# Attention loop of a decoder layer: how the moments, roots and shifts of its two normalisations are formed

## The chip, the cores and the metric

The kernel runs on one core of a Trainium2 chip. The metric is the time of one execution on the device, in microseconds.

## The reference, cut to what matters

The input x is 128 sequences of 64 rows with 128 features, fp32. A layer of three parts is computed on it, each with a layer normalisation in front:

```python
x = x + attn(_layernorm(x), wq, bq, ..., wo, bo)          # linear attention, 16 heads of 8
x = x + xattn(_layernorm(x), ctx_1024, ...)               # autocorrelation attention, 5 lags
x = x + ffn(_layernorm(x), norm_scale, w_router, ...)     # 2 of 8 experts

def _layernorm(x, axis=-1, eps=1e-05):
    m = jnp.mean(x, axis=axis, keepdims=True)
    v = jnp.var(x, axis=axis, keepdims=True)
    return (x - m) / jnp.sqrt(v + eps)
```

The first attention passes q and k through `x + 1` where x is positive and `exp(x)` elsewhere, sums the outer products of keys and values along the sequence, and divides `q * S` by `q * z`. The change concerns the first normalisation and the second.

## The kernel before, in words

The 8192 rows are 64 tiles of 128 rows (a tile is two sequences), and 4 tiles make a group, so there are 16 groups. X stays on the chip. Each engine has a program of its own, written by hand, and waits on semaphores; no planner orders the work. The attention loop goes by slots, n from -3 to 17: slots -3 to 3 and 12 to 17 are written out, slots 4 to 11 run under a loop counter, two to a turn. In a slot several groups are worked on, each at another stage (`stage(n, i, shift)` gives the group n + shift, or nothing):

- shift 3 (`z`): VectorE takes the statistics of X for the first normalisation, `bn_stats` over each of four tiles (`st_a`, line 883) and `bn_aggr` (`mv_a`, line 891), which gives mean and variance; GpSimd makes variance + eps (`ve`), its power -0.5 (`rs`, line 529), mean times root (`mr`) and 1 - that (`nb`, line 542).
- shift 2: ScalarE forms `xh = rs * x + nb` (line 688). That 1 is taken out again by the weights.
- shift 1: TensorE transposes `xh` (line 1353), ScalarE copies it (`xT`), TensorE projects tile by tile, ScalarE takes each projection out (`ex`, `rl`, `v`, lines 674 to 679), GpSimd adds `ex` and `rl` (`qk`, line 551) and forms the outer products (line 560).
- shift 0: TensorE makes the running sums (`run`), VectorE multiplies them by q (`R`, line 906) and sums them (`num`, line 916). The sums of tile 0 are made at the end of the slot before.
- shift -1 (`c`): VectorE divides (`on`, line 961), TensorE transposes `on` and projects it, VectorE adds it to X (line 969) and takes the statistics of the second normalisation (`st_c`, `mv_c`). GpSimd makes `ve_c` and `rs_c` in this slot.
- shift -2: GpSimd makes `mr_c` and `nb_c`, ScalarE forms `xh2` (line 688), TensorE transposes it and multiplies it with the projected context; ScalarE stores the result as `gd` (line 733).

The orders of VectorE and TensorE in a slot matter here. VectorE: R0, num0, reciprocal, R1, `on`, `st_a`, key products, `mv_a`, num1, sums, R2, num2, add to X, R3, `st_c`, num3, `mv_c`. TensorE: transposes of `xh`, sums 1, projection 0, key sums, projection 1, transposes of `on`, sums 2, context keys, output projection, projection 2, transposes of `xh2`, sums 3, projection 3, sums 0 of the next group, gram. In slot -3 VectorE goes on, behind the statistics of group 0, to the folding of the weights and the splitting of the biases, and only then to group 1. ScalarE in a slot: copy `xT`, projection 0, `oT`, projection 1, `xh2`, `k2T` and `x2T`, projection 2, denominators, `xh`, projection 3, `gd`. After slot 17 VectorE makes half of the last `xh2` itself (line 1041) and reduces the diagonals (line 1057).

Of the kernel before, what the change touches and what calls it, by code (L numbers as in the profile page):

```python
# [9 lines left out]
ALU = mybir.AluOpType  # L10
# [3 lines left out]
P = 128  # L14
# [52 lines left out]
def build(nc, x, ctx_t, ctx_r, wqkv_p, b_all, wo, wq2, wk2, wv2t, wo2, bq2, bk2, bv2, scale, w_router, w_experts,  # L67
          tri, stri, ident, iota, dest, walk, place, late_in, out):
    with ExitStack() as ctx:
# [48 lines left out]
        power = sb("power", [P, GT])  # L118
# [5 lines left out]
        st_a, mv_a = sb("st_a", [P, GT, 6]), [sb(f"mv_a{i}", [P, GT, 2]) for i in range(2)]  # L124
        ve_a, rs_a = sb("ve_a", [P, GT]), [sb(f"rs_a{i}", [P, GT]) for i in range(2)]
        mr_a, nb_a = sb("mr_a", [P, GT]), [sb(f"nb_a{i}", [P, GT]) for i in range(2)]
# [16 lines left out]
        st_c, mv_c = sb("st_c", [P, GT, 6]), [sb(f"mv_c{i}", [P, GT, 2]) for i in range(2)]  # L143
        ve_c, rs_c = sb("ve_c", [P, GT]), [sb(f"rs_c{i}", [P, GT]) for i in range(2)]
        mr_c, nb_c = sb("mr_c", [P, GT]), [sb(f"nb_c{i}", [P, GT]) for i in range(2)]
# [91 lines left out]
        def psum(name, banks=1):  # L237
# [18 lines left out]
        a_st, a_mv, a_ve, a_rs, a_xh = sem("a_st"), sem("a_mv"), sem("a_ve"), sem("a_rs"), sem("a_xh")  # L256
        a_ex = sem("a_ex")
        a_mr, a_nb, c_mr, c_nb = sem("a_mr"), sem("a_nb"), sem("c_mr"), sem("c_nb")
# [5 lines left out]
        c_den, c_rden, c_on, c_tr, c_oT, c_y, c_x1, c_st, c_mv, c_ve, c_rs = (  # L264
            sem(n) for n in ("c_den", "c_rden", "c_on", "c_tr", "c_oT", "c_y", "c_x1", "c_st", "c_mv", "c_ve", "c_rs"))
# [58 lines left out]
        def stage(n, i, shift):  # L324

            if i is None and not 0 <= n + shift < NG:
                return None
            return grp(n + shift, i)

# [175 lines left out]
        def _(pool):  # L505
# [12 lines left out]
            def variance(g, p, stats, seen, ve, ve_sem, rs, rs_sem, normed):  # L518

                need(pool, rs_sem, g)  # L520
                pool.wait_ge(seen, GT * g + GT)
                settle(pool)
                nc.gpsimd.tensor_scalar(ve[:], stats[p][:, :, 1], 1.0, LN_EPS, ALU.mult, ALU.add).then_inc(ve_sem, 1)

            def root(g, p, stats, seen, ve, ve_sem, rs, rs_sem, normed):

                pool.wait_ge(ve_sem, g + 1)
                need(pool, normed, GT * (g - 1))
                nc.gpsimd.tensor_tensor(rs[p][:], ve[:], power[:], ALU.pow).then_inc(rs_sem, 1)

            def mean_times_root(g, p, mv, rs, rs_sem, mr, mr_sem, nb_sem):

                pool.wait_ge(rs_sem, g + 1)
                need(pool, nb_sem, g)
                nc.gpsimd.tensor_tensor(mr[:], mv[p][:, :, 0], rs[p][:], ALU.mult).then_inc(mr_sem, 1)

            def shift(g, p, mr, mr_sem, nb, nb_sem, normed):

                pool.wait_ge(mr_sem, g + 1)
                need(pool, normed, GT * (g - 1))  # L540
                settle(pool)
                nc.gpsimd.tensor_scalar(nb[p][:], mr[:], -1.0, 1.0, ALU.mult, ALU.add).then_inc(nb_sem, 1)
# [20 lines left out]

            def slot(n, i):
                z, a1, c, d = (stage(n, i, k) for k in (3, 1, -1, -2))
                of_z = z and (z[0], z[1], mv_a, a_mv, ve_a, a_ve, rs_a, a_rs, a_xh)
                of_c = c and (c[0], c[1], mv_c, c_mv, ve_c, c_ve, rs_c, c_rs, d_xh)
# [4 lines left out]
                if d:  # L572
                    mean_times_root(d[0], d[1], mv_c, rs_c, c_rs, mr_c, c_mr, c_nb)
                    shift(d[0], d[1], mr_c, c_mr, nb_c, c_nb, d_xh)
                if a1:
                    outer_product(*a1, 0)
                    features(*a1, 1)
                    outer_product(*a1, 1)
                    features(*a1, 2)
                if z:  # L580
                    variance(*of_z)
                if a1:
                    outer_product(*a1, 2)
                if z:
                    root(*of_z)
                if a1:
                    features(*a1, 3)
                if z:
                    mean_times_root(z[0], z[1], mv_a, rs_a, a_rs, mr_a, a_mr, a_nb)
                if c:  # L590
                    variance(*of_c)
                if z:
                    shift(z[0], z[1], mr_a, a_mr, nb_a, a_nb, a_xh)
                if a1:
                    outer_product(*a1, 3)
                if c:
                    root(*of_c)
# [63 lines left out]
        def _(act):  # L661
# [23 lines left out]
            def norm(g, p, rs, nb, nb_sem, dst, dst_sem, own=GT):  # L685
                act.wait_ge(nb_sem, g + 1)
                for k in range(own):
                    nc.scalar.activation(dst[:, k, :], X[:, bass.ds(GT * g + k, 1), :].rearrange("p a b -> p (a b)"),
                                         ACT.Identity, bias=nb[p][:, k:k + 1], scale=rs[p][:, k:k + 1]).then_inc(dst_sem, 1)

            def slot(n, i):
# [1070 lines left out]
```

## Time and profile before

| | us |
|---|---|
| median of 3 runs (lowest, highest) | 621.97 (621.57, 622.45) |
| the profiled execution | 619.28 |
| its span, first to last instruction | 617.4 |
| busy: TensorE, VectorE, GpSimd, ScalarE | 553.1, 504.5, 419.3, 391.7 |

PE is TensorE's matmul, PEld its weight load, DVE VectorE, ACT ScalarE, POOL GpSimd. The span covers the profiled execution from its first instruction to its last; the execution's own time is 1.9 us longer. In a timeline row the first number is the start, the second the duration, both in us; a bracket gives the idle time of the engine just before and what ended it. Durations of neighbours on one engine overlap a little, so what an instruction costs its engine is read from its start to the next one's start. Busy shares are averages over stages that are bound by different things.

### The profile page before, as it was taken

How to read it: one execution, taken by the hardware profiler on the slowest of the kernel's cores; microseconds unless marked ns; L12 is line 12 of the kernel's file. 1: busy time of each engine (PE TensorE's matmuls, PEld its weight loads, DVE VectorE, ACT ScalarE, POOL GpSimd, SP SyncE). 2: the span in 40 equal slices, each digit the busy share in tenths (PEclk: the TensorE clock that was granted, in tenths of full speed). 3: DMA queues.
4: the chain of work that ended last, by engine and by line, in shares of the span. 5: the costliest groups of instructions: out<-in, count | busy, mean ns of one | idle time of the engine just before them, and what ended most of it. 6: DMA issues, size and time to landing. Idle time of an engine off the chain costs nothing.

```text
span 617.4 us, 16339 instructions
## 1 busy us (share of the span) xinstructions
PE 553.1 (90%) x4286; PEld 407.0 (66%) x4287; DVE 504.5 (82%) x1504; ACT 391.7 (63%) x1030; POOL 419.3 (68%) x523
## 2 busy tenths in 40 slices
PE   4888999999999997778999788999999999999993
PEld 1333444444444443455888534899999999999993
DVE  4699999999999998764588897566987878877883
ACT  3556777767667774423877412545888888878882
POOL 2999999999999995203877402763566766757762
PEclk9999999999999998989999958999999999999998
DMA  5520111111161111833666560221111111111110
GB/s 154 177 63 1 36 36 35 34 51 50 35 102 35 36 36 34 107 100 81 175 182 186 113 104 15 55 51 33 38 50 50 52 46 46 52 39 48 53 45 22
DMA packets 49976, 41.03 MB, mean 66 GB/s; under 512 B 21971, under 2 KB 40278, under 8 KB 49926
## 3 DMA queue, kind: packets, MB, share of 16 engines
q1 hardware_dynamic: 44150, 29.68, 19.7%
q0 software_dynamic: 4960, 10.49, 6.4%
q8 instruction: 23, 0.38, 0.3%
q10 hardware_dynamic: 816, 0.26, 0.2%
q14 instruction: 27, 0.22, 0.1%
HBM read 27.54 MB, written 12.88 MB: 65 GB/s over the span
## 4 chain that ended last, share of the span: by engine, by line
PE 56%; DVE 18%; issue 14%; POOL 4%; ACT 4%; DMA 2%; DVEq 1%; SPq 0%; POOLq 0%; ACTq 0%
PE bank L1349 27%; PE run L1349 23%; DVE R L906 3%; PE bank L1353 3%; ACT xs L787 2%; PE run L1616 2%; DVE on L961 2%; DVE st_c L883 1%; DVE mean_early L1057 1%; POOL shared L560 1%; PE run L1540 1%; POOL qk L551 1%; DVE mv_c L891 1%; ACT xrT L773 1%; DVE shared L1236 1%
## 5 line engine op out<-in xcount | busy, mean ns | idle before, releaser
L634 POOL DMA_INDIRECT shared<-xs_d,row_u x91 | 87.7, 964 | 61.8 <-DVE row_u L1247 31.0
L560 POOL TENSOR_TENSOR shared<-v,qk 128x1024 f32<-128x1024 f32 x64 | 125.0, 1953 | 4.8 <-POOL qk L551 2.5
L641 POOL DMA_INDIRECT out_x<-shared x64 | 63.4, 991 | 48.2 <-DVE shared L1319 21.0
L906 DVE TENSOR_TENSOR R<-run,qk 128x1024 f32<-128x1024 f32 x64 | 77.4, 1210 | 9.2 <-PE run L1349 8.4
L916 DVE TENSOR_REDUCE num<-R 128x128 f32<-128x1024 f32 x64 | 77.3, 1208 | 1.5
L1349 PE MATMUL bank<-wqkv,xT 128*64 128x128 f32 (+1 forms) x384 | 69.1, 348 | 9.0 <-ACT v L677 8.2
L1349 PEld LDWEIGHTS bank<-wqkv,xT 128*64 128x64 f32 (+1 forms) x384 | 33.4, 158 | 61.7 <-issue 30.1
L1349 PE MATMUL run<-shared,tris_s 64*64 64x512 f32 x512 | 71.4, 628 | 0.0
L816 ACT ACTIVATE shared<-run,scale_s 128x128 f32<-128x128 f32 (+1 forms) x78 | 30.0, 385 | 41.4 <-PE run L1616 41.4
L551 POOL TENSOR_TENSOR qk<-ex,rl 128x256 f32<-128x256 f32 x64 | 46.6, 728 | 2.5 <-ACT ex L679 2.4
L674 ACT ACTIVATE ex<-bank 128x256 f32<-128x256 f32 x64 | 24.3, 380 | 30.7 <-PE bank L1349 27.6
L1349 PE MATMUL run<-w_s,hid 128*128 (+1 forms) x312 | 41.4, 275 | 0.0
L1349 PE MATMUL bank<-w_s,hid 128*128 (+1 forms) x308 | 41.0, 276 | 0.4 <-issue 0.4
L820 ACT ACTIVATE ct<-w_s 128x512 f32 x64 | 39.8, 621 | 0.2 <-issue 0.2
L1340 DVE TENSOR_TENSOR hid<-run,shared 128x256 f32<-128x256 f32 x78 | 32.9, 422 | 7.3 <-ACT shared L826 7.1
L1349 PEld LDWEIGHTS run<-w_s,hid 128*128 128x128 f32 x312 | 38.0, 192 | 0.1
L1349 PEld LDWEIGHTS bank<-w_s,hid 128*128 128x128 f32 x308 | 37.5, 192 | 0.8 <-issue 0.6
L826 ACT ACTIVATE shared<-run 128x256 f32<-128x256 f32 x78 | 29.8, 383 | 11.1 <-PE run L1349 8.1
L826 ACT ACTIVATE shared<-bank 128x256 f32<-128x256 f32 x77 | 29.5, 383 | 10.2 <-PE bank L1349 7.8
L706 ACT ACTIVATE oT<-bank 128x512 f32<-128x512 f32 x16 | 9.6, 597 | 39.6 <-PE bank L1353 39.6
L1340 DVE TENSOR_TENSOR hid<-bank,shared 128x256 f32<-128x256 f32 x77 | 32.4, 421 | 2.1 <-ACT shared L826 1.9
L1349 PE MATMUL run<-shared,ct 128*128 128x128 f32 x256 | 33.9, 275 | 0.0
(275 smaller groups left out, 1432.9 us busy)
## 6 DMA issues: line engine op xcount, KB each, us to landing
xs_d<-xs SPq DMA_DIRECT2D x16, 270.0 KB, 5.1
X<-in_x SPq DMA_DIRECT2D x16, 256.0 KB, 2.8
ct<-in_ctx_t SPq DMA_DIRECT2D x16, 256.0 KB, 2.9
ct<-in_ctx_r SPq DMA_DIRECT2D x16, 256.0 KB, 3.7
gram_d<-gd SPq DMA_DIRECT2D x14, 256.0 KB, 2.4
w_s<-in_w_experts SPq DMA_DIRECT2D x8, 384.0 KB, 3.9
circ<-prob_d SPq DMA_DIRECT2D x30, 64.0 KB, 2.7
shared<-xs_d,row_u POOLq DMA_INDIRECT x91, 2.6
```

Of the source, the lines that this page charges most:

```text
L551: nc.gpsimd.tensor_tensor(qk[p][:, k, :], ex[k % 2][:], rl[k % 2][:], ALU.add).then_inc(a_f, 1)
L560: nc.gpsimd.tensor_tensor(outer[k].rearrange("p (h e d) -> p h e d", h=H, e=D), vv.unsqueeze(3).broadcast_to([P, H, D, D]), kk.unsqueeze(2 ...
L634: nc.gpsimd.indirect_dma_start(xg[q], None, xs_d[:, :], bass.IndirectOffsetOnAxis(ap=rows, axis=0)).then_inc(xg_in[q], 16)
L641: nc.gpsimd.indirect_dma_start(out[:, :], bass.IndirectOffsetOnAxis(ap=xg[(NXI + j) % NX][:, DEST:DEST + 1].bitcast(U32), axis=0), yg[q], ...
L674: nc.scalar.activation(ex[k % 2][:], bank[1][:, HALF:HALF + 2 * E], ACT.Relu, scale=-1.0).then_inc(a_pev, 1)
L816: nc.scalar.activation(xgT[p][:, cols], bank[0][:, cols], ACT.Copy, scale=scale_s[:, 0:1]).then_inc(x_xT, 1)
L820: nc.scalar.activation(w_tile[n % 2][0], w_s[:, dyn(held[0] * W_E, 2 * HID)], ACT.Copy).then_inc(x_wa, 1)
L826: nc.scalar.activation(silu[p][h], bank[1 + 2 * p + h][:, HID:2 * HID], ACT.Silu).then_inc(x_silu, 2 // len(items_of(i, up[0])))
L906: nc.vector.tensor_tensor(R[:, 0:D * E].rearrange("p (h e d) -> p h e d", h=H, e=D), run[k % 2][:].rearrange("p (h e d) -> p h e d", h=H, ...
L916: nc.vector.tensor_reduce(num[p][:, k, :], R[:, 0:D * E].rearrange("p (x d) -> p x d", d=D), AX.X, ALU.add).then_inc(b_red, 1)
L1340: nc.vector.tensor_tensor(hid[p][h][:], bank[1 + 2 * p + h][:, 0:HID], silu[p][h], ALU.mult).then_inc(x_h, 2 // len(items_of(i, j)))
L1349: return nc.tensor.matmul(o, l, r, start=start, stop=stop, skip_group_check=True)
```

## The change

The statistics of both normalisations of a slot lie in one tile now, `st[:, h]` with h = 0 for the first and 1 for the second, and so do `mv`, `rs` and `nb`. `bn_stats` gives count, mean and count times variance of two halves of a row. In place of `bn_aggr` for each tile, VectorE takes the difference of the halves' means and the sum of both fields, in two instructions over the slot's eight tiles. ScalarE forms the square of half the difference and the sum's second field / 128 + eps, and GpSimd adds the two, takes the root, and forms the shift. The moments come once a slot, at its end (in slots without a second normalisation, at the place of `mv_a`). ScalarE's part and GpSimd's whole chain stand in the next slot: on ScalarE behind the copy of `xT`, on GpSimd the root first and the shifts behind the first `qk`. Slots at either end handle one half only.

```diff
@@ VectorE
             def moments(at, p, own, seen):
+                dve.wait_ge(m_st, seen)
+                need(dve, m_mr, at + 2)
                 settle(dve)
-                for k in range(GT):
-                    nc.vector.bn_aggr(mv[p][:, k, :], st[:, k, :]).then_inc(mv_sem, 1)
+                nc.vector.tensor_tensor(df[p][:, own, :, 0], st[:, own, :, 1], st[:, own, :, 4], ALU.subtract).then_inc(m_mv, 1)
+                nc.vector.tensor_tensor(mv[p][:, own], st[:, own, :, 1:3], st[:, own, :, 4:6], ALU.add).then_inc(m_mv, 1)
...
                 if b:
                     key_dots(*b)
-                if z:
-                    moments(z[0], z[1], st_a, a_st, mv_a, a_mv, a_mr, 1)
+                if m and not c:
+                    moments(*m, stats_before(n + 1, i))
...
                 if b:
                     sum_heads(*b, 3)
                 if c:
-                    moments(c[0], c[1], st_c, c_st, mv_c, c_mv, c_mr, 1)
+                    moments(*m, stats_before(n + 1, i))
@@ ScalarE, slot
                 m = moment_slot(n, i, -1)
...
                 if a1:
                     a_evac_xT(*a1)
+                if m:
+                    deviations(*m)
                 if a1:
                     a_evac_proj(*a1, 0)
@@ ScalarE
+            def deviations(at, p, own):
+
+                act.wait_ge(m_mv, 2 * (at + 3) + 2)
+                need(act, m_ve, at + 3)
+                nc.scalar.activation(sq[:, own], df[p][:, own, :, 0], ACT.Square, scale=0.5).then_inc(m_sq, 1)
+                nc.scalar.activation(me[:, own], mv[p][:, own, :, 1], ACT.Copy, bias=LN_EPS, scale=1.0 / E).then_inc(m_sq, 1)
@@ GpSimd
+            def root(at, p, own):
+
+                pool.wait_ge(m_sq, 2 * (at + 3) + 2)
+                need(pool, m_rs, at + 3)
+                nc.gpsimd.tensor_tensor(ve[:, own], sq[:, own], me[:, own], ALU.add).then_inc(m_ve, 1)
+                pool.wait_ge(m_ve, at + 4)
...
+                nc.gpsimd.tensor_tensor(rs[p][:, own], ve[:, own], power[:, own], ALU.pow).then_inc(m_rs, 1)
+
+            def shifts(at, p, own):
+
+                pool.wait_ge(m_rs, at + 4)
+                need(pool, m_nb, at + 3)
+                nc.gpsimd.tensor_tensor(mr[:, own], mv[p][:, own, :, 0], rs[p][:, own], ALU.mult).then_inc(m_mr, 1)
+                pool.wait_ge(m_mr, at + 4)
                 settle(pool)
+                nc.gpsimd.tensor_scalar(nb[p][:, own], mr[:, own], -0.5, 1.0, ALU.mult, ALU.add).then_inc(m_nb, 1)
@@ GpSimd, slot
+                m, a1 = moment_slot(n, i, -1), stage(n, i, 1)
                 if i is None and n == -1:
                     pool.wait_ge(bias_ch, 8)
+                if m:
+                    root(*m)
                 if a1:
                     features(*a1, 0)
+                if m:
+                    shifts(*m)
                 if a1:
                     outer_product(*a1, 0)
+                    for k in range(1, GT):
+                        features(*a1, k)
+                        outer_product(*a1, k)
```

Removed with it are `variance`, `mean_times_root` and `shift` on GpSimd, whose calls stood between the outer products. `moment_slot(n, i, shift)` gives the slot number `at`, its parity and the halves it holds.

## Rows read from the trace of the kernel before

**Rows 1.** Stretches of two slots: length, busy us (instructions) per engine, clock, DMA.

```profile
core 0: us, PE busy (x) PEld busy (x) DVE busy (x) ACT busy (x) POOL busy (x), PEclk, DMA share, GB/s
119.79:134.17 14.38, 13.43 (x103) 6.71 (x100) 14.21 (x30) 10.26 (x31) 13.59 (x17) 1.00 0.13 36
220.81:235.26 14.45, 13.53 (x102) 6.66 (x99) 13.18 (x23) 9.57 (x29) 12.10 (x13) 1.00 0.12 37
```

**Rows 2.** Timeline without `st_a`: start, us, engine, line, operation, xcount [idle before].

```profile
219.60 1.22 DVE L906 TENSOR_TENSOR R<-run,qk 128x1024 f32<-128x1024 f32 x1 [1.20 <-PE run L1349]
...
226.87 0.67 DVE L961 TENSOR_TENSOR on<-num,bank 128x512 f32<-128x512 f32 x1
...
227.69 0.63 PE L1353 MATMUL bank<-id_s,on 128*128 128x128 f32 x4 [0.54 <-DVE on L961]
...
234.05 1.23 DVE L906 TENSOR_TENSOR R<-run,qk 128x1024 f32<-128x1024 f32 x1 [1.20 <-PE run L1349]
```

**Rows 3.** Timeline of a slot inside the counted loop, VectorE.

```profile
118.65 1.22 DVE L906 TENSOR_TENSOR R<-run,qk 128x1024 f32<-128x1024 f32 x1
...
121.69 0.37 DVE L891 BATCH_NORM_AGGREGATE mv_c<-st_c 128x2 f32<-128x6 f32 x4
...
121.98 1.19 DVE L906 TENSOR_TENSOR R<-run,qk 128x1024 f32<-128x1024 f32 x1
...
127.88 0.37 DVE L891 BATCH_NORM_AGGREGATE mv_a<-st_a 128x2 f32<-128x6 f32 x4
```

**Rows 4.** Timeline of the expert stage, a small tensor_tensor and its follower.

```profile
442.76 0.16 DVE L1335 TENSOR_TENSOR gt<-eq 128x2 f32<-128x2 f32 x1
442.84 0.42 DVE L1340 TENSOR_TENSOR hid<-run,shared 128x256 f32<-128x256 f32 x1
```

**Rows 5.** Groups by line, GpSimd: xcount, busy us, mean ns, idle before.

```profile
L529 POOL TENSOR_TENSOR rs_c<-ve_c,power 128x4 f32<-128x4 f32 x16 | 16.4, 1028 | 0.2
...
L535 POOL TENSOR_TENSOR mr_c<-mv_c,rs_c 128x4 f32<-128x4 f32 x16 | 3.2, 201 | 0.2
```

**Rows 6.** Timeline of the slot of rows 3, GpSimd, ScalarE and TensorE.

```profile
117.63 1.95 POOL L560 TENSOR_TENSOR shared<-v,qk 128x1024 f32<-128x1024 f32 x1 [0.33 <-POOL qk L551]
...
119.54 0.73 POOL L551 TENSOR_TENSOR qk<-ex,rl 128x256 f32<-128x256 f32 x1
...
124.40 0.38 ACT L674 ACTIVATE ex<-bank 128x256 f32<-128x256 f32 x1 [1.50 <-PE bank L1349]
...
129.32 1.65 ACT L688 ACTIVATE xh<-X,nb_c,rs_c 128x128 f32 x4 [0.30 <-POOL nb_c L542]
...
131.29 0.66 PE L1353 MATMUL bank<-id_s,xh 128*128 128x128 f32 x4
```

**Rows 7.** Groups by line, ScalarE: a small activation and the table load.

```profile
L688 ACT ACT_TABLE_LOAD x1 | 1.3, 1283 | 0.6 <-PEq L1753 0.6
...
L779 ACT ACTIVATE gap_e<-gap 128x16 f32<-128x16 f32 (+2 forms) x5 | 1.0, 202 | 3.2 <-DVE gap L1116 3.2
```

**Rows 8.** Timeline of the start, slots -1 and 0.

```profile
12.81 0.38 ACT L674 ACTIVATE ex<-bank 128x256 f32<-128x256 f32 x1 [2.01 <-PE bank L1349]
...
13.84 0.38 DVE L891 BATCH_NORM_AGGREGATE mv_a<-st_a 128x2 f32<-128x6 f32 x4 [0.15 <-DVE st_a L883]
...
16.46 1.84 PE L1349 MATMUL bank<-wqkv,xT 128*128 128x256 f32 x6 [0.93 <-ACT v L677]
...
19.45 1.85 PE L1349 MATMUL bank<-wqkv,xT 128*128 128x256 f32 x6 [1.14 <-ACT v L677]
...
23.29 1.23 DVE L906 TENSOR_TENSOR R<-run,qk 128x1024 f32<-128x1024 f32 x1 [4.11 <-PE run L1349]
...
25.98 1.23 DVE L906 TENSOR_TENSOR R<-run,qk 128x1024 f32<-128x1024 f32 x1 [0.22 <-PE run L1349]
```

**Rows 9.** Timeline of the loop's end.

```profile
258.71 0.60 ACT L733 ACTIVATE gd<-bank 128x512 f32<-128x512 f32 x1 [0.79 <-PE bank L1349]
...
259.39 0.22 POOL L523 TENSOR_SCALAR ve_c<-mv_c 128x4 f32<-128x4 f32 x1 [4.63 <-issue]
```

More of the change, by code:

```diff
@@ L117, in build @@
         vo3 = sb("vo3", [P, E], BF16)
-        power = sb("power", [P, GT])
+        power = sb("power", [P, 2, GT])
         X = sb("X", [P, NT, E])
-        st_a, mv_a = sb("st_a", [P, GT, 6]), [sb(f"mv_a{i}", [P, GT, 2]) for i in range(2)]
-        ve_a, rs_a = sb("ve_a", [P, GT]), [sb(f"rs_a{i}", [P, GT]) for i in range(2)]
-        mr_a, nb_a = sb("mr_a", [P, GT]), [sb(f"nb_a{i}", [P, GT]) for i in range(2)]
+        st = sb("st", [P, 2, GT, 6])
+        mv, df = ([sb(f"{n}{i}", [P, 2, GT, w]) for i in range(2)] for n, w in (("mv", 2), ("df", 1)))
+        sq, me, ve, mr = (sb(n, [P, 2, GT]) for n in ("sq", "me", "ve", "mr"))
+        rs, nb = ([sb(f"{n}{i}", [P, 2, GT]) for i in range(2)] for n in ("rs", "nb"))
         xh = sb("xh", [P, GT, E])
@@ L328, in stage, with moment_slot, stats_before @@
             return grp(n + shift, i)
+        def moment_slot(n, i, shift):
+            at = n + shift if i is None else 2 * i + n + shift
+            if i is not None:
+                return at, (n + shift) % 2, slice(0, 2)
+            if not -3 <= at <= NG:
+                return None
+            return at, at % 2, slice(0 if at + 3 < NG else 1, 2 if at >= 1 else 1)
+        def stats_before(n, i):
+            if i is not None:
+                return 2 * GT * (2 * i + n + 1)
+            return GT * (min(n + 3, NG) + min(max(n - 1, 0), NG))
         def pairs(eng, count, body):
@@ L516, in _ @@
             pool.wait_ge(setup, 3)
-            def variance(g, p, stats, seen, ve, ve_sem, rs, rs_sem, normed):
-                need(pool, rs_sem, g)
-                pool.wait_ge(seen, GT * g + GT)
-                settle(pool)
[L523 to L542, printed above, removed]
+            def root(at, p, own):
[3 more added lines that the diff above has]
+                pool.wait_ge(m_ve, at + 4)
+                if isinstance(at, int):
+                    need(pool, a_xh, GT * min(at + 2, NG))
+                    need(pool, d_xh, GT * (at - 2))
+                else:
+                    pool.wait_ge(a_xh, GT * (at + 2))
+                    pool.wait_ge(d_xh, GT * (at - 2))
+                nc.gpsimd.tensor_tensor(rs[p][:, own], ve[:, own], power[:, own], ALU.pow).then_inc(m_rs, 1)
[4 more added lines that the diff above has]
+                pool.wait_ge(m_mr, at + 4)
+                settle(pool)
+                nc.gpsimd.tensor_scalar(nb[p][:, own], mr[:, own], -0.5, 1.0, ALU.mult, ALU.add).then_inc(m_nb, 1)
             def features(g, p, r, k):
@@ L711, in slot @@
                     need(act, d_tr, g)
-                    norm(g, p, rs_c, nb_c, c_nb, xh2, d_xh, GT // 2 if i is None and g == NG - 1 else GT)
+                    norm(g, m[0], m[1], 1, xh2, d_xh, GT // 2 if i is None and g == NG - 1 else GT)
                 if d:
@@ L725, in slot @@
                     need(act, a_tr, g)
-                    norm(g, p, rs_a, nb_a, a_nb, xh, a_xh)
+                    norm(g, m[0], m[1], 0, xh, a_xh)
                 if a1:
@@ L972, in slot @@
             def slot(n, i):
-                z, b, c = (stage(n, i, k) for k in (3, 0, -1))
+                z, b, c, m = *(stage(n, i, k) for k in (3, 0, -1)), moment_slot(n, i, 0)
                 if b:
@@ L1013, in slot @@
                     dve.wait_ge(c_x1, c[0] + 1)
-                    stats(c[0], c[1], st_c, c_st, mv_c, c_mv, c_mr, 1)
+                    stats(c[0], m[0], 1)
                 if b:
```

62 lines of the change are left out of this document (15 added, 47 removed).

## The prediction, made before the changed kernel was run

> **What bounds the kernel now.** I read the stretches first. A slot of the attention loop lasts 14.4 us, with VectorE busy 14.21, GpSimd 13.59 and TensorE 13.43 [rows 1]: three engines nearly full, so a share of busy time decides nothing. The other stretch shows the same 14.45 us for a late slot that has no first-normalisation statistics left: VectorE has a full microsecond less to do (13.18) and nothing got faster. So not VectorE's sum but a ring sets the pace. The timeline of such a slot shows it [rows 2]: the multiply `R` of tile 3 starts at 219.60, then come `st_c`, a reduction, `mv_c`, the next slot's first tiles, and `on` ends at 227.54; TensorE transposes `on` at 227.69, runs on without a gap to the running sums of tile 3, and the next such `R` starts at 234.05. 7.94 on VectorE, 0.15 to hand over, 6.36 on TensorE: 14.45. In the slots before, VectorE alone needs the same 14.4: 14.21 busy of 14.38, and `R`, `mv_c` and `mv_a` show no wait [rows 1, 3]: two bounds with one length. `mv_c` lies in both, `mv_a` only in VectorE's sum, since it comes after `on`.
>
> **Aggregates.** Four aggregations take 0.29 from start to the next start (121.69 to 121.98), and the two groups last the same 0.37 [rows 3]. In their place stand two tensor_tensor instructions over 8 and 16 numbers, or 4 and 8 in slots with one half. The small tensor_tensor `gt` on VectorE shows 0.16 busy, but the next instruction starts 0.08 behind it [rows 4]. From below the pair is two aggregations' worth, 0.145; from above two full durations, 0.32. I take 0.09 a piece, 0.18, nearest to `gt`, since nothing in the pair waits for the other. A slot's ring is then 0.29 - 0.18 = 0.11 shorter (between 0.15 shorter and 0.03 longer), VectorE's own sum 0.58 - 0.18 = 0.40 shorter. After it the ring is 14.33 and VectorE's sum 14.03, so the ring decides and 0.29 of each 0.40 is worth nothing. `mv_a` pays once, in slot 1, where the ring doesn't close yet: 0.29. Slots 0 to 15 have a moments step on the path: 16 x 0.11 = 1.76, and with slot 1 2.05 us in all (bounds 2.7 and -0.2).
>
> **GpSimd.** Its chain also turns around in 14.4. Per slot one `ve`, `mr` and `nb` go (each 0.28 with its gap) and one of two roots. The roots now hold 8 numbers: 4 take 1.028, while a multiply of 4 takes 0.201 [rows 5]. So the rise x lies between 0 and 2 x 0.827 + 0.201 - 1.028 = 0.83 if every number costs alike, 1.03 if the whole duration doubles; I take 0.83. The new order also loses cover: an instruction right behind the one it needs pays its delay (0.33 idle before the outer product at 117.63) [rows 6], today once a slot, then three times, and `ve` to `rs` stands bare too. Sum: outer products 4 x 1.91, `qk` to outer 3 x 1.02, `qk` to `mr` 0.68, `mr` to `nb` to outer 0.64, `ve` to `rs` 0.5, root 0.99 + x: 13.5 + x, so 14.34 with x = 0.83, beside a ring of 14.33. It just fits, and the lead of 2 us and more that outer products have on the running sums can take a few hundredths per slot. I put it at 0, upper bound 2.6 (below).
>
> The rule that speaks against the change stands in the Trainium skill, GPSIMD Engine Reference, in the key structural facts: eight cores of 16 lanes serve the 128 partitions, so numbers that lie side by side in a partition are taken one after another. By it the root of 8 costs the 0.83 more; without it GpSimd would gain 0.8 us of air a slot and my forecast would stay, since the ring decides either way. No row of before has a root of another width.
>
> The shifts come in time: from `qk` of tile 2 (119.54) on, the new order reaches the end of `nb` 8.69 + x later, 129.1; today ScalarE's normalisation waits 0.30 for `nb_c` and starts at 129.32, ends at 130.97, and the transposes that want it start at 131.29 [rows 6].
>
> **ScalarE.** It gets a square and a copy over 8 numbers each; the nearest row is one over at most 16, 0.202 [rows 7], which follow each other after about 0.15. They stand behind the copy of `xT`, where ScalarE waits 1.50 us for a projection, from 122.90 to 124.40 [rows 6], and the moments they need are there before (`mv_c` ends at 122.06 [rows 3]). Cost 0 in a steady slot; without that cover 0.3 each.
>
> A page that would make it dear is ScalarE: Activation LUTs in the Trainium skill, section on table sets: a function outside the loaded set calls for a load, about 2.7 us with its drain by that page. By it a square outside the set would be two loads in each of 20 slots, over 100 us; the same page counts cheap functions as fillers of every set. The trace holds one load, 1.28 us, at the normalisation's first activation, and none inside the loop of relu, exp, identity and copy [rows 7].
>
> **The start is where it costs.** In slot -1 ScalarE's deviations come behind `xT` and ahead of the first projection's evacuation, and they need the moments of group 1. These lie behind VectorE's bias chain: `mv_a` starts at 13.84 [rows 8]. Today ScalarE starts that evacuation at 12.81. Then: the pair done 14.05, square and copy 14.1 to 14.4, evacuation at 14.4, so 1.6 late. Everything of TensorE in this slot hangs on it (projection 2 follows `v` at 16.46, idle 0.93). Projection 3 today waits 1.14 instead, 0.21 more, since `v` was held by GpSimd; that falls away, as GpSimd's chain for group 1 (one half, 4 numbers, x = 0) ends where it does now. That leaves 1.4 at VectorE's first `R` of slot 0, at 23.29 today after 4.11 idle. From there VectorE hardly pauses, so the delay passes on whole, but for 0.2: the second `R`, at 25.98, waited 0.22 for TensorE, and by then more work lies behind that TensorE can prepare meanwhile. I take +1.2, bounds 0 (something else covers it) and 1.9 (six matmuls last 1.84 there [rows 8], and their faster pace may come later too).
>
> **The end.** The last normalisation's chain gains a stop. Today `ve_c` starts at 259.39, 0.27 behind the aggregates. ScalarE is in `gd` from 258.71 to 259.31 [rows 9], and the deviations queue behind it: square 259.3, copy to 259.7, `ve` at 259.75. +0.35 on the chain that leads to the selection of lags; bounds 0.15 and 0.6.
>
> **Sum.** -2.05 + 0 + 0 + 1.2 + 0.35 = -0.5 us. Against the profiled execution's 619.28 us (span 617.4) this is 618.8. The median of the runs is 621.97, 2.69 above the profiled one, so I forecast 621.5 there. Its own bounds: terms at their good ends -2.6, at their bad ends about +2.7, rarely all together: 620.2 to 622.9.
>
> **Rivals.**
> 1. *VectorE is the real bound and the ring has slack.* For: its brackets are empty in the loop [rows 3]. Against: 14.45 in the slot with 13.18 of work [rows 1]. It would save 0.40 in twelve slots and 0.11 in four, 5.2 in all: 621.97 - 5.2 + 1.55 = 618.3. Chance 0.08.
> 2. *The start is absorbed.* ScalarE's wait costs nothing since some other step of the start is what VectorE waits for: -2.05 + 0.35 gives 620.3. For: DMA still loads X and weights then, and GpSimd's work there is long too. Against: each projection waits for ScalarE. Chance 0.20.
> 3. *GpSimd becomes the bound (the other side).* If x is 1.03 or the bare waits cost 0.1 more each, its round is 14.6 to 14.7 in the eight slots that run under a loop counter. Deciding point: the round passes 14.33 and the leads are used up, first at the shifts, where ScalarE has only about 0.3. Price up to 8 x 0.33 = 2.6: 624.1. For: three waits laid bare. Against: lead elsewhere. Chance 0.14, half of it with a price that only cancels the gain.
> 4. *The start costs more than 1.9*, or the stops on ScalarE delay what follows in each slot (0.1 a slot): 623.5. Chance 0.13.
> 5. *A table is loaded for the square,* and back for the next exponential: 2 x 20 x 1.28 = 51 us more [rows 7], 673. Against: one load serves the loop so far. Chance 0.02.
>
> **Chances.** Forecast 0.43. About 0.2%, 1.24 us, is what a measurement of this kernel tells from no change. Faster by more: rival 1 whole, rival 2 in two thirds, the good tail of the forecast 0.08, together 0.30. Slower by more: half of rival 3, rival 4 and 5, a tail of 0.03, together 0.25. Same 0.45. Range 619.8 to 623.8, with 0.1 below and 0.1 above.
>
> **What would show it.** Right: the time between two `R` of tile 3 falls from 14.4 to about 14.3, and VectorE then shows a wait of about 0.3 on TensorE in every slot; the first evacuation starts near 14.4 and the first `R` near 24.6; `ve` of the last slot comes near 0.6 behind the pair. Wrong: a slot of 14.03 (rival 1), a first `R` at 23.3 (rival 2), an empty bracket all through GpSimd and ScalarE waiting over 0.5 for `nb` (rival 3), a root of 8 at 1.0 (x = 0). A pair over 0.29 between starts would overturn the sign of the largest term.

## The result, and the profile after it

The changed kernel takes 626.27 us (median of 4 runs, 626.05 to 626.92); the kernel before took 621.77 (620.85 to 622.45, 4 runs) beside it. The ratio is 1.0075, with a 95% interval of 1.0058 to 1.0093: slower by 0.75%, where 621.5 and 619.8 to 623.8 were forecast. Taken once more later, in 7 runs beside 24 of the kernel before, it is 626.11 against 620.50, ratio 1.0086 (1.0053 to 1.0119). The profiled execution of the changed kernel (626.37, span 624.5) lies at its median, that of before 2.7 below its own, so the traces differ by 7.1 us of span and the medians by 4.5. One execution is left out of the times below: a sixth one of the kernel with the common chain alone took 1826.31 us, where its other five lie between 625.74 and 627.23.

The stretches of the attention loop come first: the eight slots that run under the loop counter together, one of them ([rows 1] has the same slot of before), and the two stretches from the first addition to `X` (slot 1) to the second and to the third. A stretch here runs from one addition to `X` to the next.

```profile
core 0: us, PE busy (x) PEld busy (x) DVE busy (x) ACT busy (x) POOL busy (x), PEclk, DMA share, GB/s
92.00:210.99 118.99, 108.91 (x796) 53.30 (x800) 115.30 (x186) 82.87 (x257) 102.50 (x97) 1.00 0.19 45
121.78:136.62 14.84, 13.59 (x103) 6.65 (x107) 14.41 (x24) 10.32 (x33) 12.62 (x13) 1.00 0.12 35
...
47.44:61.50 14.06, 11.46 (x65) 5.81 (x65) 13.84 (x25) 7.90 (x25) 13.55 (x13) 0.88 0.00 1
61.50:77.40 15.90, 14.91 (x113) 7.39 (x115) 14.01 (x23) 10.34 (x33) 12.51 (x13) 1.00 0.11 34
```

The same eight slots and the same two stretches of the kernel before:

```profile
89.03:204.31 115.28, 107.82 (x796) 53.59 (x792) 113.70 (x233) 82.32 (x241) 108.68 (x129) 1.00 0.20 46
...
45.87:60.05 14.18, 11.88 (x79) 5.94 (x82) 14.11 (x30) 8.25 (x25) 13.58 (x17) 1.00 0.01 1
60.05:74.50 14.45, 13.53 (x103) 6.67 (x99) 14.21 (x30) 10.14 (x31) 13.49 (x17) 1.00 0.13 37
```

A counted slot went from 14.41 (115.28 / 8) to 14.87 us (118.99 / 8), at full clock; GpSimd got 0.8 us a slot lighter (108.68 to 102.50 over the eight), and VectorE has 47 instructions fewer in these slots (186 for 233) and 1.6 us more busy time. Something of VectorE's got longer. Its timeline at the slot's end, and GpSimd's of the same moment, show what:

```profile
124.73 1.20 DVE L917 TENSOR_REDUCE num<-R 128x128 f32<-128x1024 f32 x1
125.85 0.73 DVE L891 TENSOR_TENSOR df<-st 128x8 f32<-128x8 f32 x1
126.50 0.16 DVE L892 TENSOR_TENSOR mv<-st 128x16 f32<-128x16 f32 x1
126.58 1.21 DVE L907 TENSOR_TENSOR R<-run,qk 128x1024 f32<-128x1024 f32 x1
...
124.59 1.96 POOL L569 TENSOR_TENSOR shared<-v,qk 128x1024 f32<-128x1024 f32 x1 [0.24 <-POOL qk L560]
126.50 0.76 POOL L560 TENSOR_TENSOR qk<-ex,rl 128x256 f32<-128x256 f32 x1
```

The difference of eight numbers is recorded as busy for 0.73 us, and the next instruction starts at 126.50: the moment at which GpSimd's outer product, begun at 124.59, makes room for GpSimd's next. The sums of sixteen numbers right behind it show 0.16 and cost 0.08, as `gt` did in [rows 4]. So the pair takes 0.73 from `df` to `R` where the four aggregates took 0.29 [rows 3]. All eight counted slots are alike. In the slots that are written out the outer product started earlier and the wait is shorter:

```profile
67.05 0.31 DVE L891 TENSOR_TENSOR df<-st 128x8 f32<-128x8 f32 x1
...
65.38 1.95 POOL L569 TENSOR_TENSOR shared<-v,qk 128x1024 f32<-128x1024 f32 x1
```

`df` costs the 0.08 of the forecast where GpSimd stands still, where its outer product is just ending (51.06, below), and once beside a root: at 15.63 it shows 0.17, while GpSimd's root runs from 15.07 to 16.08. So not every GpSimd instruction holds it up.

On the slot's ring, VectorE's `R` of tile 3 now waits 0.36 for TensorE in each counted slot, as the forecast wanted it for a ring that is longer than VectorE's own work:

```profile
122.81 1.22 DVE L907 TENSOR_TENSOR R<-run,qk 128x1024 f32<-128x1024 f32 x1 [0.36 <-PE run L1350]
```

GpSimd's root in its two widths, by groups (xcount, busy us, mean ns, idle before), is 0.63 longer with eight numbers:

```profile
L542 POOL TENSOR_TENSOR rs<-ve,power 128x8 f32<-128x8 f32 x12 | 19.8, 1647 | 2.9 <-POOL ve L534 2.6
...
L542 POOL TENSOR_TENSOR rs<-ve,power 128x4 f32<-128x4 f32 x8 | 8.1, 1016 | 0.6
```

The start, to be held against [rows 8]: ScalarE waits for the moments of group 1 and begins the first evacuation at 14.55, and VectorE's first two `R` follow late. The first line below is ScalarE's.

```profile
14.34 0.20 ACT L679 ACTIVATE sq<-df 128x4 f32<-128x4 f32 x1 [3.51 <-DVE mv L892]
...
14.55 0.36 ACT L664 ACTIVATE ex<-bank 128x256 f32<-128x256 f32 x1
...
24.79 1.23 DVE L907 TENSOR_TENSOR R<-run,qk 128x1024 f32<-128x1024 f32 x1 [7.49 <-PE run L1350]
27.81 1.23 DVE L907 TENSOR_TENSOR R<-run,qk 128x1024 f32<-128x1024 f32 x1 [0.55 <-PE run L1350]
```

Slots 1 and 2 of the changed kernel, VectorE, ScalarE and TensorE:

```profile
51.06 0.16 DVE L891 TENSOR_TENSOR df<-st 128x8 f32<-128x8 f32 x1
...
51.34 0.21 ACT L679 ACTIVATE sq<-df 128x8 f32<-128x8 f32 x1 [1.15 <-DVE mv L892]
...
51.95 1.13 PE L1350 MATMUL bank<-qk,tris_s 128*128 128x256 f32 x4 [0.46 <-POOL qk L560]
...
56.02 0.63 PE L1354 MATMUL bank<-id_s,on 128*128 128x128 f32 x4 [2.13 <-DVE on L962]
...
57.76 2.08 PE L1350 MATMUL bank<-ct,wkk 128*128 128x512 f32 x2
...
64.01 1.23 DVE L907 TENSOR_TENSOR R<-run,qk 128x1024 f32<-128x1024 f32 x1 [1.82 <-PE run L1350]
```

and the lines that answer to TensorE's and the last one before the change:

```profile
51.70 1.13 PE L1349 MATMUL bank<-qk,tris_s 128*128 128x256 f32 x4 [1.39 <-POOL qk L551]
...
54.54 0.63 PE L1353 MATMUL bank<-id_s,on 128*128 128x128 f32 x4 [0.92 <-DVE on L961]
...
56.12 1.12 PE L1349 MATMUL bank<-ct,wkk 128*128 128x512 f32 x2
...
60.90 1.22 DVE L906 TENSOR_TENSOR R<-run,qk 128x1024 f32<-128x1024 f32 x1 [0.17 <-PE run L1349]
```

TensorE waited 1.39 and 0.92 before and now waits 0.46 and 2.13: about the same idle time, but most of it in one piece. GpSimd's `qk` no longer comes late; that this makes the second piece long is my reading, and a short first wait alone doesn't do it (0.38 and 1.37 in the kernel with the first probe, below). Behind the longer piece the same two matmuls take 2.08 instead of 1.12. That is the lower of the clock's two levels: the granted clock is 0.50 from 57.70 to 59.90, and 0.88 over the whole stretch, where it was 1.00 before. VectorE meets the lost time later, at the `R` at 64.01, for which it waits 1.82 instead of 0.17, and the next stretch lasts 15.90 for 14.45.

By the starts of `X` and of `mean_early`, the first large reduction behind the loop, the loop's end comes 8.32 us later. The start gives +1.57 (first addition to `X` at 47.44 for 45.87), the stretch behind it -0.12, the next +1.45, the one ahead of the counted slots +0.07, the eight counted slots +3.71, the two behind them +0.36, the last full one +1.32 (TensorE ran slow in it for longer than before), and the rest -0.04. The stages behind the loop took 1.2 us less than in the trace of before.

### The profile page after: what moved, and what is told of

It is laid out like the page before. It is cut to its first block, busy times and chain, and to the rows that moved or that the text cites. A ratio compares the mean times of both kernels' runs of the same rounds, so it can differ in the third digit from the quotient of the medians.

```text
span 624.5 us, 16196 instructions
## 1 busy us (share of the span) xinstructions
PE 555.4 (89%) x4286; PEld 409.8 (66%) x4287; DVE 503.7 (81%) x1416; ACT 394.4 (63%) x1070; POOL 410.0 (66%) x475
## 4 chain that ended last, share of the span: by engine, by line
PE 54%; issue 18%; DVE 15%; POOL 4%; ACT 3%; DMA 3%; DVEq 1%; SPq 1%; POOLq 0%; ACTq 0%
PE bank L1350 27%; PE run L1350 22%; DVE R L907 3%; PE bank L1354 2%; ACT xs L787 2%; PE run L1617 2%; DVE st L883 2%; POOL qk L560 1%; DVE on L962 1%; DVE mean_early L1058 1%; PE run L1541 1%; DMA ct<-in_ctx_r 1%; DMA shared<-xs_d,row_u 1%; DVE num L917 1%; ACT xrT L773 1%
## 5 line engine op out<-in xcount | busy, mean ns | idle before, releaser
L685 ACT ACTIVATE xh<-X,nb,rs 128x128 f32 (+1 forms) x126 | 52.0, 500 | 4.4 <-POOL nb L551 4.4
L664 ACT ACTIVATE ex<-bank 128x256 f32<-128x256 f32 x64 | 24.3, 380 | 24.7 <-PE bank L1350 24.6
```

## Experiments

All are told against the kernel before on the same chip. The slot time is the mean of the eight counted slots in the profile.

**A small tensor_tensor added to the kernel before, where the pair would stand.** Its result is read by nobody.

```
                 if c:
                     moments(c[0], c[1], st_c, c_st, mv_c, c_mv, c_mr, 1)
+                if c:
+                    nc.vector.tensor_tensor(pr[:, 0], st_c[:, :, 1], st_c[:, :, 4], ALU.subtract).then_inc(probed, 1)
```

> The kernel before with one more VectorE instruction at the end of a slot, behind mv_c: a tensor_tensor over 4 numbers with both operands in SBUF, result unused. Theory P (such an instruction on VectorE doesn't start before the GpSimd instruction under way has ended): in the counted slots GpSimd's outer product ends about 0.5 us behind mv_c, so the probe shows 0.5 to 0.6 us there, lies in the ring and makes a slot 14.9 to 15.0 instead of 14.43; time 626 to 630. Theory Q (the first small instruction behind register waits in the counted slots is slow, or the strided operands are): the probe has no wait of its own and follows aggregates, so it shows 0.16 busy and 0.08 to the next start, a slot of 14.5, time 622 to 623.5.

Measured: 624.34 (623.79 to 626.05) against 621.03, ratio 1.0068 (1.0043 to 1.0093). The slot is the one expected, the time lies under the 626 to 630. One instruction of four numbers, in a kernel that is otherwise the one before, costs most of what the change costs (3.3 us between medians, against 4.5). Its line, and the outer product beside it:

```profile
124.14 0.55 DVE L1022 TENSOR_TENSOR pr<-st_c 128x4 f32<-128x4 f32 x1
...
122.71 1.96 POOL L562 TENSOR_TENSOR shared<-v,qk 128x1024 f32<-128x1024 f32 x1
```

122.71 + 1.96 = 124.67, and the probe ends at 124.69. Slots last 14.90. The wait needs neither the new chain nor the wide root. In one slot the same probe meets GpSimd's root of four numbers instead and does not wait, and the probe of the next run passes beside it too (0.14 at 51.81, with the root from 51.58 to 52.60):

```profile
50.14 1.02 POOL L531 TENSOR_TENSOR rs_a<-ve_a,power 128x4 f32<-128x4 f32 x1
50.38 0.13 DVE L1022 TENSOR_TENSOR pr<-st_c 128x4 f32<-128x4 f32 x1
```

**The same with one operand.** The line is `nc.vector.tensor_scalar(pr[:, 0], st_c[:, :, 1], 1.0, 0.0, ALU.mult, ALU.add)`.

> The same probe at the same place with one operand in SBUF: a tensor_scalar over the same 4 numbers with the same stride. Theory P: 0.08 to the next start in every slot, no dependence on GpSimd, time about 1.2 us above before (16 x 0.08). Theory Q: the same as the probe with two operands, whatever that shows.

Measured: 624.41 (623.17 to 626.64), ratio 1.0063 (1.0039 to 1.0088), slots of 14.89. My theory fell in this part: I had put the wait down to the second operand.

```profile
125.55 0.55 DVE L1022 TENSOR_SCALAR pr<-st_c 128x4 f32<-128x4 f32 x1
...
124.12 1.95 POOL L562 TENSOR_TENSOR shared<-v,qk 128x1024 f32<-128x1024 f32 x1
```

**The same as a reduction,** `nc.vector.tensor_reduce(pr[:, 0], st_c[:, :, 1:3], AX.X, ALU.add)`.

> The kernel before with one small instruction of VectorE at the end of each slot, behind the aggregates: a tensor_reduce that adds two numbers of each of four tiles (SBUF to SBUF), where the two probes before it had a tensor_tensor and a tensor_scalar. Theory P' (tensor_tensor and tensor_scalar with all operands in SBUF wait for the instruction that GpSimd has under way; reductions do not): the probe takes at most 0.16 and 0.1 to the next start in every slot although GpSimd's outer product runs on beside it, a counted slot stays at 14.43 + 0.1, about 14.5, and the time is 621.0 + 1.0 to 1.6 = 622.0 to 622.6. Rival Q' (any small VectorE instruction at this place waits, the place and not the form decides): 0.55 and 0.47 to the next start in the counted slots, as with the other two, slots of 14.9, 624.4.

Measured: 621.88 (620.88 to 624.60, 12 runs) against 620.16, ratio 1.0025 (1.0008 to 1.0042), just under the 622.0 to 622.6 expected; slots of 14.48. The outer product runs from 122.11 to 124.06, and the probe starts and ends in its middle:

```profile
123.54 0.13 DVE L1022 TENSOR_REDUCE pr<-st_c 128x4 f32<-128x8 f32 x1
123.58 1.22 DVE L908 TENSOR_TENSOR R<-run,qk 128x1024 f32<-128x1024 f32 x1
...
122.11 1.95 POOL L562 TENSOR_TENSOR shared<-v,qk 128x1024 f32<-128x1024 f32 x1
```

Same place, same source, same neighbour: the form of the instruction decides. The large `R` right behind it, which takes one operand from PSUM, does not wait either.

The Trainium skill has this in SBUF — State Buffer, section "Who interferes with whom": VectorE and GpSimd share one pair of SBUF ports as an exclusive lock, and whoever comes second waits for the whole instruction of the first. It counts among the contenders a VectorE instruction with two SBUF inputs (against a GpSimd instruction that reads SBUF) and tensor_scalar or a copy in a two-port mode, and says of tensor_reduce on trn2 that it never contends. The three probes agree: 0.46 to 0.48, 0.46 to 0.47 and 0.04 to 0.05 to the next start in the counted slots; that the tensor_scalar ran in a two-port mode no trace shows. The root doesn't fit: it is a tensor_tensor that reads SBUF, and the probes beside it at 50.38 and 51.81, and `df` at 15.63, did not wait for its end. Why is open.

**The pair ahead of the last reduction.** In the changed kernel the moments move 1.1 us forward, into the beginning of the outer product.

```
+                if c:
+                    moments(*m, stats_before(n + 1, i))
                 if b:
                     sum_heads(*b, 3)
-                if c:
-                    moments(*m, stats_before(n + 1, i))
```

> The changed kernel with the pair ahead of the slot's last reduction instead of behind it. Theory P: there GpSimd's outer product has just begun (it starts 0.15 us before) so df waits 1.5 to 1.8 us for its end in the counted slots instead of 0.65; the slot grows from 14.88 to about 15.8, time 632 or more, unless GpSimd's phase against VectorE shifts with it; in any case each df whose stretch is long ends together with a GpSimd instruction. Theory Q: df costs 0.65 wherever it stands, plus up to 0.18 for the statistics it follows, slot 15.0 to 15.1, time 628.

Measured: 657.42 (656.40 to 658.88), ratio 1.0603 (1.0576 to 1.0629).

```profile
102.08 1.57 DVE L891 TENSOR_TENSOR df<-st 128x8 f32<-128x8 f32 x1 [0.18 <-DVE st L883]
103.57 0.16 DVE L892 TENSOR_TENSOR mv<-st 128x16 f32<-128x16 f32 x1
...
101.67 1.96 POOL L569 TENSOR_TENSOR shared<-v,qk 128x1024 f32<-128x1024 f32 x1 [0.24 <-POOL qk L560]
```

The wait is what is left of the outer product: it began 0.41 earlier, and `df` holds VectorE for 1.5. The time is far more than sixteen such waits. A slot lasts 17.17, TensorE waits 2.06 to 2.20 for `on` in each counted one (0.81 to 0.92 in the changed kernel), and the granted clock over them is 0.94 instead of 1.00. That the longer waits bring the slow clock was not tried by itself.

**ScalarE's square and copy behind the first evacuation, in slots -1 and 2.**

```
-                if m:
+                late = i is None and n in (-1, 2)
+                if m and not late:
                     deviations(*m)
                 if a1:
                     a_evac_proj(*a1, 0)
+                if m and late:
+                    deviations(*m)
```

> The changed kernel with ScalarE's square and copy behind the evacuation of projection 0 instead of ahead of it, in slots -1 and 2 alone. Theory S (the start costs since ScalarE stands still for the moments of group 1, and slot 2 for those of slot 1): VectorE's first R comes back from 24.8 to about 23.4, the slow-clock episode at 57 us goes as TensorE no longer waits 2.1 us there, together 2 to 3 us less than the changed kernel: 623.3 to 624.5. Rival (the start is bound by GpSimd's chain for group 1 and ScalarE's wait is hidden): no change, 626.3.

Measured: 626.64 (624.13 to 627.95, 5 runs) against 621.03, ratio 1.0111 (1.0091 to 1.0131). The trace does what I expected at the start, first `R` at 23.26 instead of 24.79, and the median does not: a miss. The stretch of 15.90 is there as in the changed kernel, for TensorE waits even longer for `on`:

```profile
55.11 0.63 PE L1357 MATMUL bank<-id_s,on 128*128 128x128 f32 x4 [2.75 <-DVE on L965]
...
57.39 2.07 PE L1353 MATMUL bank<-ct,wkk 128*128 128x512 f32 x2
```

The profiled execution was the fastest of the five, so its shorter loop must not be taken for the median's.

**The common chain alone: aggregates kept.** Eight of them stand where the pair stood. The places of ScalarE's two activations and of GpSimd's chain stay; both activations are copies now that each give half of variance + eps, and the shift's factor is -1.0 for -0.5.

```
-                nc.vector.tensor_tensor(df[p][:, own, :, 0], st[:, own, :, 1], st[:, own, :, 4], ALU.subtract).then_inc(m_mv, 1)
-                nc.vector.tensor_tensor(mv[p][:, own], st[:, own, :, 1:3], st[:, own, :, 4:6], ALU.add).then_inc(m_mv, 1)
+                for h in range(own.start, own.stop):
+                    for k in range(GT):
+                        ins = nc.vector.bn_aggr(mv[p][:, h, k, :], st[:, h, k, :])
+                ins.then_inc(m_mv, 2)
```

> The changed kernel with the common chain kept and the two instructions of moments replaced by eight aggregations at the same place (the two activations of ScalarE give half of variance plus epsilon each). Theory P': the aggregations do not wait for GpSimd: 8 x 0.072 = 0.57 from the first to the instruction behind them, against 0.73 for the pair in a counted slot and 0.32 in a slot written out, so counted slots of 14.43 + 0.28 = 14.7, the start as in the changed kernel (first R near 24.8) and the end alike: about 625 (624 to 626.3), a second below the changed kernel at most. Rival R (the chain on GpSimd and ScalarE, not the pair, makes the slots long): counted slots stay at 14.88 or get longer by the difference of the two forms' own lengths, 626.5 or more.

Measured: 626.38 (625.74 to 627.23, 5 runs) against 620.16, ratio 1.0093 (1.0072 to 1.0114). The slot went as expected (14.67; 0.55 from the aggregates to `R`, no wait), the total came 0.1 above the upper end of what I gave it. So the pair is not the whole loss: without its wait the slots are still longer than before's, since eight aggregates now stand on the ring where four did, and the stretch behind the second `X` lasted 16.12, after a wait of 2.51 for `on`.

```profile
126.00 0.63 DVE L893 BATCH_NORM_AGGREGATE mv<-st 128x2 f32<-128x6 f32 x8
126.55 1.19 DVE L909 TENSOR_TENSOR R<-run,qk 128x1024 f32<-128x1024 f32 x1
```

**The difference on GpSimd, the sums as one reduction.** GpSimd can't be in its own way, and the reduction doesn't wait.

```
+            def differences(at, p, own, seen):
+                pool.wait_ge(m_st, seen)
+                need(pool, m_sq, 2 * (at + 1))
+                nc.gpsimd.tensor_tensor(df[p][:, own, :, 0], st[:, own, :, 1], st[:, own, :, 4], ALU.subtract).then_inc(m_df, 1)
...
                         features(*a1, k)
+                        if k == GT - 1 and now:
+                            differences(*now, stats_before(n + 1, i))
                         outer_product(*a1, k)
...
+                act.wait_ge(m_df, at + 4)
...
+                nc.vector.tensor_reduce(mv[p][:, own].rearrange("p h k w -> p (h k) w"),
+                                        st[:, own].rearrange("p h k (s w) -> p (h k) w s", s=2)[:, :, 1:3, :], AX.X, ALU.add).then_inc(m_mv, 2)
```

> The changed kernel with the difference of the halves' means computed by GpSimd (between the features and the outer product of tile 3, 0.28 more there each slot) and VectorE's sums of means and squares in one tensor_reduce over 16 pairs. Theory P': nothing of VectorE waits for GpSimd at the slot's end, the reduction takes 0.1 to 0.15 from its start to the next, a counted slot lasts 14.43 - 0.29 + 0.12 = 14.26, GpSimd's round (14.0 to 14.3 with the added instruction) just fits; against before 16 x -0.17 = -2.7, start +1.5, end +0.35, so 620.2 (618.7 to 622). Rival R: the slots do not go below 14.4 since GpSimd's chain is too long with one more instruction: 622.5 to 625. A reduction of 0.5 or more would bring theory P' down.

Measured: 621.52 (619.40 to 623.53, 12 runs) against 620.16, ratio 1.0012 (0.9995 to 1.0029): no difference from the kernel before that can be told, and 4.6 us less than the changed kernel (626.11, on another chip; the two ratios to the kernel before say 4.6 too). The slot is 14.36, so the reduction took less off than the 0.17 I expected: in seven of the eight slots `R` starts 0.21 behind it.

**The same with the late start.**

> The kernel of the run before with ScalarE's square and copy behind the evacuation of projection 0 in slots -1 and 2, as in the run with the late start. Theory P': first R near 23.3 instead of 24.8, slots of 14.26 as there; 618.7 to 620, faster than both kernels, if the gain at the start is kept. The run with the late start did not keep it (TensorE waited longer for the normalised output in slot 2 and its clock fell there), so a rival S gives it back in slot 2: then as the run before, 620.2.

Measured: 618.83 (616.22 to 622.39, 12 runs), ratio 0.9981 (0.9961 to 1.0001). The first `R`, expected near 23.3, came at 24.40 all the same (24.38 in the run before). Yet the median is 2.7 below that of the run before, on the same chip, so what the late start gained here did not come through the first `R`. Why the first `R` stayed, ScalarE's timeline says:

```profile
4.98 1.28 ACT L690 ACT_TABLE_LOAD   x1 [4.82 <-POOL df L548]
6.28 0.20 ACT L690 ACTIVATE sq<-df 128x4 f32<-128x4 f32 x1
```

In the two kernels with two waits ahead of the square, the load of the loop's table came only when the data were there. In the others it starts at 0.73 or 0.74, under the wait for X.

**Its two waits split:** the square waits for the difference, the copy for the sums.

```
-                act.wait_ge(m_mv, 2 * (at + 3) + 2)
                 act.wait_ge(m_df, at + 4)
                 nc.scalar.activation(sq[:, own], df[p][:, own, :, 0], ACT.Square, scale=0.5).then_inc(m_sq, 1)
+                act.wait_ge(m_mv, 2 * (at + 3) + 2)
```

> The kernel with the difference on GpSimd and the late start, its two waits on ScalarE split: the square waits for the difference alone, the copy for the sums. In the run before both waits stood ahead of the square, and the one table load (1.28) started only behind them, at 4.98, so that everything of the first slots came 1.3 late (xT at 11.54 where the kernel before has 10.21). Theory T (that load was the whole of it): the load goes back under the wait for X, xT at 10.2 to 10.3, first R at 23.1 to 23.3, median 618.83 - 1.2 = 617.6 (616.6 to 618.6), faster than the kernel before (620.2) by 0.4%. Rival S (something else keeps the first R at 24.4): 618.8.

Measured: 618.34 (616.26 to 621.74, 12 runs) against 620.50, ratio 0.9968 (0.9944 to 0.9991): faster than both kernels. The square starts at 4.80, and the first `R` at 22.82:

```profile
22.82 1.23 DVE L922 TENSOR_TENSOR R<-run,qk 128x1024 f32<-128x1024 f32 x1 [4.18 <-PE run L1365]
...
120.14 0.18 DVE L906 TENSOR_REDUCE mv<-st 128x16 f32<-128x32 f32 x1
120.35 1.23 DVE L922 TENSOR_TENSOR R<-run,qk 128x1024 f32<-128x1024 f32 x1
```

Of the 1.6 us gained at the first `R` against the run before, the medians, taken on two chips, show 0.5, and the profiled executions (617.25 and 617.44) 0.2. Between these two the rest went in the last full stretch, 15.26 in this trace and 14.31 in the one before, with TensorE's clock low for a while, and in the one behind it, 9.15 and 8.45; where the medians lost it isn't known.

**The split without the late start.**

> The same with the split waits and without the late start. Theory T: xT at 10.2 again, but ScalarE now stands at the square until VectorE's sums of group 1 (13.7), so that the first evacuation starts at 14.1 and the first R at 24.3, as with the table load exposed: the two delays lie beside each other, and only with both gone does the first R come to 23.2. Median 620 to 621.5, against 617.6 for the run with the late start. Rival S': first R at 23.3 here too, 618.

Measured: 620.14 (618.03 to 622.89, 12 runs), ratio 0.9988 (0.9965 to 1.0010), first `R` at 24.47. For the first `R` it is as theory T had it: the exposed load and the wait at the square lay beside each other (24.38 with both, 24.40 and 24.47 with one of them, 22.82 with none). For the time it isn't: the late start alone took 2.7 us off, and here, with the split in place, it is worth 1.8 between medians whose executions spread over 5 us.

**The changed kernel again.**

> The changed kernel once more, on the chip of these runs and in more executions. If the four executions taken before it stand for it: 1.0075 times the kernel before, so 624.5 to 626.5 here, df at 0.72 in the counted slots. Its trace shows how much of the 16 slots repeats (counted slots of 14.88) and how much is the clock of TensorE in slots 2 and 15, which differed from trace to trace by up to 1.5 us each.

Measured: 626.11 (623.74 to 628.18), ratio 1.0086. In its trace `df` is 0.73 in the counted slots again, the stretch behind the second `X` takes 15.91 after a wait of 2.54 for `on`, and the last full one 16.76: the two places of the slow clock repeat. The stretch behind the first `X`, however, took 15.75 here and 14.06 in the first trace.

## Why the prediction was wrong

The slot's ring was read rightly, and its size is the best-tested number of the case. What stands between the last reduction and the next `R` goes one for one into a slot:

| kernel | slot's end, us | mean counted slot | 14.41 + end - 0.29 |
|---|---|---|---|
| before | 0.29 | 14.41 | |
| difference on GpSimd | 0.21 | 14.36 | 14.33 |
| reduction as probe | 0.34 | 14.48 | 14.46 |
| chain alone, 8 aggregates | 0.55 | 14.67 | 14.67 |
| changed kernel | 0.73 | 14.87 | 14.85 |
| tensor_tensor as probe | 0.76 | 14.90 | 14.88 |

VectorE's own sum can't give these slots: without `mv_a` it would be 14.41 - 0.58 + 0.73 = 14.56 in the changed kernel and 14.38 in the chain alone, where 14.87 and 14.67 were measured. So rival 1 fell.

- **Aggregates: the step that failed.** "I take 0.09 a piece, 0.18, nearest to `gt`, since nothing in the pair waits for the other." Nothing in the pair waits for the other, but its first instruction waits for GpSimd. The row that I took the price from [rows 4] stands in the expert stage, and I did not ask what GpSimd did beside it: it was issuing an indirect DMA (from 442.25 to 443.22, the line below), beside which `gt` did not wait. In the loop GpSimd is busy for 13.59 of a slot's 14.38 [rows 1], mostly with outer products, so a small instruction of VectorE seldom meets it free. The bound "from above two full durations, 0.32" held in no counted slot. In place of -0.11 a slot stands +0.46, and in place of -2.05 in all +3.7 for the eight counted slots alone. The sentence that a pair over 0.29 would turn the sign of the largest term came true. The rule for it was in the Trainium skill (SBUF — State Buffer, the section named above), and I weighed another one, on the number of cores behind GpSimd, in its place.

```profile
442.25 0.97 POOL L634 DMA_INDIRECT shared<-xs_d,row_u  x1 [0.30 <-issue]
```

- **GpSimd: right in sign, mis-sized.** x is 1.647 - 1.016 = 0.63, not 0.83. GpSimd is not the bound: it waits in every counted slot for ScalarE's exponential (0.59 to 1.12; 0.98 before the `qk` at 123.62), so rival 3 fell. By the rule of the Trainium skill weighed there (GPSIMD Engine Reference, key structural facts) a wider root costs more, and the trace agrees with the direction, while its size lies below my 0.83.
- **ScalarE: right.** The square and the copy take 0.20 each and cost nothing in a steady slot; no table is loaded for the square. "The trace holds one load" was misread: there is a second one, at 388.38 in the kernel before, far behind the loop, and the changed kernel has two as well.
- **The start: the steps right, the worth open.** First evacuation at 14.55 (14.4 forecast), first `R` at 24.79 (24.6), and in this trace +1.57 at the first addition to `X` (+1.2, bounds 0 and 1.9). One trace doesn't fix that number: in the second trace of the changed kernel the first addition starts at 46.27, only 0.40 after before's, and the probes, whose first `R` comes at 23.1 to 23.4 as before, have it from 46.42 to 47.86. In the medians the late start gave nothing in the changed kernel (626.64), and 2.7 and 1.8 us in the kernels with the difference on GpSimd, in the first of these without moving the first `R`. So it can't be added as a plain term.
- **The end: mis-sized.** Time from the statistics to the last rows' normalisation went from 4.03 to 4.17, +0.14, just under the lower bound of 0.15, where +0.35 was taken. `ve` starts 0.25 later behind the first instruction of the moments, and the last root takes 1.01 instead of 1.19.
- **Not in the sum at all: TensorE's clock.** +1.45 near the start and +1.32 in the last full stretch. In twelve traces (all kernels here but the one with the pair moved forward, 55 us into the span) the wait for `on`, the two matmuls behind it and VectorE's later wait go together: 0.92 to 1.62, then 1.12 or 1.13, then 0.17 to 0.43 in eight of them; 2.13 to 2.75, then 2.07 or 2.08, then 1.82 in the other four. These four are the kernels that have the new chain and counted slots that end with 0.5 or more (the changed kernel twice, with the late start, and the chain alone). That the freed `qk` of GpSimd joins two waits of TensorE into one is read from the traces and was not tried by itself. What makes the last full stretch slow in some (16.5 to 16.8 in four traces, 14.3 to 15.5 in the other eight) stays open. It isn't the length of the wait alone: TensorE waits 2.67 to 2.88 for `on` there in all twelve, and the two matmuls behind take 1.12 in two of them and 1.53 to 2.07 in ten. Nor does it need the slow slots: the two kernels with the difference on GpSimd and without the late start have it too. With a wait of the same 2.84, first the changed kernel, then the one with the late start:

```profile
249.13 1.12 PE L1354 MATMUL bank<-id_s,on 128*128 128x128 f32 x4 [2.84 <-DVE on L962]
...
252.09 2.07 PE L1350 MATMUL bank<-ct,wkk 128*128 128x512 f32 x2
```

```profile
248.30 0.65 PE L1357 MATMUL bank<-id_s,on 128*128 128x128 f32 x4 [2.84 <-DVE on L965]
...
249.91 1.12 PE L1353 MATMUL bank<-ct,wkk 128*128 128x512 f32 x2
```

## What to carry to other kernels

Before a small VectorE instruction with all operands in SBUF is put on the critical path, look at what GpSimd runs at that moment: it can cost the rest of GpSimd's instruction, here up to 1.5 us for eight numbers, whatever its own length is. GpSimd's outer products and sums of `ex` and `rl` cost it, its root of four numbers did not. Statistics, aggregates, reductions and instructions with an operand in PSUM went through beside the outer product. So fewer instructions is not the measure: at the slot's end eight aggregates (0.55) beat two tensor_tensors (0.73), and one reduction (0.21) beat both, once the difference was moved to GpSimd itself. In the whole kernel's time only the reduction showed: the kernel with eight aggregates was no faster than the changed one.

## What the runs showed of the hardware

- A VectorE tensor_tensor or tensor_scalar from SBUF to SBUF ends with the GpSimd outer product (1.95) that was running when it came: 0.55 where 0.13 was its length, 0.73 and 1.57 where it was 0.16. Beside GpSimd's root of four numbers (1.02) it did not wait (0.13, 0.14 and 0.17). The wait is recorded as busy time, so no bracket shows it.
- A root (pow) on GpSimd costs 1.016 for 4 numbers a partition and 1.647 for 8, so by these two widths an estimate of 0.16 a number beside a fixed 0.4.
- The load of ScalarE's table was hidden under a wait with one semaphore ahead of the activation and exposed (1.28) with two.
